# Four layers on one core: values turned by VectorE and through DRAM, values' products one projection later, position tables stationary with the queries moving

## Time and profile before

| | |
|---|---|
| median of 3 runs | 1244.69 us (1243.16 to 1244.88) |
| the profiled execution, its own time | 1246.36 us |
| its span | 1244.4 us |
| PE / PEld busy | 1216.4 us (98%) / 975.0 us (78%) |
| DVE / ACT / POOL busy | 690.4 us (55%) / 475.1 us (38%) / 641.5 us (52%) |
| chain that ended last | PE 89%, DVE 5%, ACT 2% |
| DMA | 155.03 MB, mean 125 GB/s |

### The profile page before, as it was taken

One profiled execution on the slowest core, in us unless ns is written; L12 is line 12 of the kernel. 1 busy time (PEld: TensorE's weight loads), 2 busy tenths in 40 slices (PEclk: granted clock), 3 DMA queues, 4 the chain that ended last, 5 costly groups with the idle time before them and its releaser, 6 DMA issues.

```text
span 1244.4 us, 19555 instructions
## 1 busy us (share of the span) xinstructions
PE 1216.4 (98%) x6768; PEld 975.0 (78%) x6768; DVE 690.4 (55%) x1434; ACT 475.1 (38%) x1229; POOL 641.5 (52%) x726
## 2 busy tenths in 40 slices
PE   6999999999999999999999999999999999889998
PEld 4788896478888888888888878777887787668887
DVE  7534444775665433666452578756347776476212
ACT  3611141034645320656341164644206555243212
POOL 4633389256565567555546655555665556464000
PEclk9999999999999999999999999999999999999999
DMA  5211124025564643454645356557535565620012
GB/s 185 84 46 48 34 56 117 8 65 160 154 169 137 184 134 97 127 177 128 185 136 166 86 160 212 180 160 223 168 102 151 175 209 156 205 60 1 29 40 68
DMA packets 129376, 155.03 MB, mean 125 GB/s; under 512 B 30080, under 2 KB 84000, under 8 KB 129280
## 3 DMA queue, kind: packets, MB, share of 16 engines
q1 hardware_dynamic: 118976, 146.92, 39.7%
q10 hardware_dynamic: 10304, 6.88, 1.8%
HBM read 111.81 MB, written 37.75 MB: 120 GB/s over the span
## 4 chain that ended last, share of the span: by engine, by line
PE 89%; DVE 5%; ACT 2%; issue 1%; DMA 1%; SPq 1%; POOL 0%; ACTq 0%; DVEq 0%; POOLq 0%
PE PS L1137 53%; PE PS L682 7%; PE PS L1758 7%; PE PS L1183 4%; PE PS L960 3%; PE PS L969 2%; PE PS L975 2%; PE PS L1227 2%; PE PS L1216 2%; PE PS L1775 2%; PE PS L1247 2%; PE PS L665 1%; PE PS L1197 1%; DVE bst L257 1%; PE PS L700 1%
## 5 line engine op out<-in xcount | busy, mean ns | idle before, releaser
L1137 PE MATMUL PS<-XB,w_hi 128*128 128x512 f32 x1024 | 340.5, 397 | 1.2 <-POOL w_lo L228 1.2
L226 POOL CAST w_hi<-w_raw 128x512 fp32r<-128x512 f32 x195 | 124.2, 637 | 307.5 <-PE PS L1137 213.0
L228 POOL TENSOR_TENSOR w_lo<-w_raw,w_hi 128x512 fp32r<-128x512 f32 x195 | 256.1, 1313 | 15.6
L1137 PEld LDWEIGHTS PS<-XB,w_hi 128*128 128x128 f32 x1024 | 192.2, 188 | 47.1 <-issue 5.0
L1137 PE MATMUL PS<-XB,w_lo 128*128 128x512 f32 x512 | 200.2, 391 | 0.0
L1137 PE MATMUL PS<-XB,part 128*128 128x512 f32 x768 | 190.3, 394 | 0.0
L1137 PEld LDWEIGHTS PS<-XB,part 128*128 128x128 f32 x768 | 141.9, 188 | 32.2 <-issue 2.3
L1373 ACT ACTIVATE part<-PS,nmax 128x256 f32<-128x256 f32 (+1 forms) x256 | 112.2, 443 | 141.6 <-DVE nmax L1485 93.2
L1383 ACT ACTIVATE part<-part,prec 128x256 f32<-128x256 f32 (+1 forms) x256 | 105.8, 476 | 27.7 <-DVE prec L1500 27.7
L228 POOL TENSOR_TENSOR part<-part,part 128x512 fp32r<-128x512 f32 x85 | 111.5, 1312 | 6.8
L1137 PE MATMUL PS<-part,w_hi 128*128 128x512 f32 x344 | 112.9, 395 | 1.5 <-DVE part L1544 1.5
(11 more groups left out here) (136 smaller groups left out, 1884.0 us busy)
## 6 DMA issues: line engine op xcount, KB each, us to landing
w_raw<-in_w SPq DMA_DIRECT2D x187, 256.0 KB, 2.8
part<-in_w SPq DMA_DIRECT2D x85, 256.0 KB, 2.8
turned<-part SPq DMA_DIRECT2D x128, 128.0 KB, 2.9
part<-turned SPq DMA_DIRECT2D x32, 512.0 KB, 5.0
turned<-part SPq DMA_DIRECT2D x128, 96.0 KB, 2.5
part<-turned SPq DMA_DIRECT2D x32, 384.0 KB, 4.0
strips<-part ACTq DMA_DIRECT2D x16, 256.0 KB, 2.7
out_x<-xT SPq DMA_DIRECT2D x16, 256.0 KB, 2.1
```

The source lines that it names most:

```text
L226: pool.tensor_copy(hi, raw).then_inc(w_hi_done, 1)
L228: pool.tensor_tensor(lo, raw, hi.bitcast(F32), ALU.subtract).then_inc(w_ready, 1)
L1137: m = nc.tensor.matmul(PS[:, bank, :], wt[:, (c % 4) * P:(c % 4) * P + P], rhs(hl, c), start=c == k == 0, stop=c == CK - 1 and k == 2)
```

## The change

- Values: PE's four transposes per item (32 items) go, and so does ACT's copy in front of them. DVE transposes the values from PSUM in 32 x 32 squares (`turn_values`), SP writes them to a new DRAM tensor in four DMAs and reads them back in one (`values_to_dram`, `values_from_dram`), and ACT copies them into `v` (`take_v`), within the next item. The bias of the values in layer 2 is added after their product instead.
- Order on PE: keys of i + 1, values of i, values' product of i - 1, queries of i + 2, and the eight output blocks after these queries instead of before them. Weights are listed in that order.
- Position products: 24 matmuls of 64 columns per item of layer 2 become three of 512 columns, the tables stationary and the queries moving in permuted order. The result lies with positions on the partitions. DVE transposes it (`turn_relative`) and ACT stores it in four DMAs instead of one, right behind the first exponentials; its two copies L1407 go.
- `rest_of_o` and `evac_o` stand behind the normalization, `norm.coefficients` moves from j = 0 to j = 1; at j = 0 the queries of i + 2 are read out ahead of the output blocks' sums.
- Probabilities go out in four DMAs per item instead of eight, of twice the size, and come back in two.
- The end: six output blocks instead of three are begun ahead of the last values' product, in six banks, and `build_m` has other banks and places (`M_AFTER`).

```diff
--- before.py
+++ after.py
             take_block(i, "V", range(0 if i else 1, 2))
+            if i + 2 < ITEMS:
+                take_block(i + 2, "Q")
             if s and j == 0:
                 for o in range(CK):
                     take((s - 1, "O", o), STAGES[s - 1][0], "O", o)
-            if i + 2 < ITEMS:
-                take_block(i + 2, "Q")
-            for o in {ITEMS - 2: (0,), ITEMS - 1: (1, 2)}.get(i, ()):
...
-    vT = carve(13312, [P, HALF])
+    vB = carve(13312, [P, 4 * P])
...
-    probB = [carve(at, [P, 4 * N]) for at in (14848, 11264)]
+    probB = carve(11264, [P, 8 * N])
...
-        def turn_values(i):
-            pe.wait_ge(v_evac, i + 1)
-            if turned_bank(i) == S:
-                pe.wait_ge(p_exp, 4 * i + 1)
-            else:
-                pe.wait_ge(rel_evac, 2 * (ITEMS - LO_KEYS))
-            if i:
-                pe.wait_ge(v_ready, i)
-            for tt in range(4):
-                m = nc.tensor.transpose(PS[:, turned_bank(i), tt * P:tt * P + P], vT[:, tt * P:tt * P + P], ident[:, :])
-            m.then_inc(v_tr, 1)
...
             if i == ITEMS or layer_of(i) == 1:
                 return
             pe.wait_ge(q_hi, i + 1)
             pe.wait_ge(q_lo, i + 1)
...
             pe.wait_ge(tables_ready, 1)
-            for tt in range(4):
-                for k, (x, y) in enumerate(((qh[i % 2], rel_hi), (qh[i % 2], rel_lo), (ql[i % 2], rel_hi))):
-                    for hh in range(2):
-                        rows = slice(64 * hh, 64 * hh + 64)
-                        to = PS[:, REL[hh], 64 * tt:64 * tt + 64].rearrange("p (t n) -> p t n", t=2)
-                        m = nc.tensor.matmul(to, x[rows, tt * P:tt * P + P], y[rows, :, 32 * hh:32 * hh + 32],
-                                             start=k == 0, stop=k == 2)
-                        if (tt, k) == (3, 2):
-                            m.then_inc(rel_done, 1)
+            for k, (x, y) in enumerate(((rel_hi, qh[i % 2]), (rel_lo, qh[i % 2]), (rel_hi, ql[i % 2]))):
+                m = nc.tensor.matmul(PS[:, X, :], x.rearrange("p r n -> p (r n)"), y.rearrange("p (a y x) -> p y a x", a=2, y=SIDE),
+                                     start=k == 0, stop=k == 2)
+            m.then_inc(rel_done, 1)
...
+        project(2, "Q", range(CK))
         for i in range(1, LAST - 1):
             score_block(i)
             project(i + 1, "K", range(CK))
+            project(i, "V", range(CK))
             attend(i - 1, 0)
             attend(i - 1, 1)
-            project(i, "V", range(CK))
+            project(i + 2, "Q", range(CK))
             if i % PAIRS == 0:
                 s = i // PAIRS - 1
-                out_block(s, 0, range(CK))
-                out_block(s, 1, range(0, 2))
-                turn_values(i)
-                out_block(s, 1, range(2, CK))
-                for o in range(2, CK):
+                for o in range(CK):
                     out_block(s, o, range(CK))
-                project(i + 2, "Q", range(CK))
-            else:
-                project(i + 2, "Q", range(0, 2))
-                turn_values(i)
...
         score_block(i)
         project(LAST, "K", range(CK))
+        project(i, "V", range(CK))
         attend(i - 1, 0)
         attend(i - 1, 1)
-        project(i, "V", range(CK))
         scores(LAST, 0)
         scores(LAST, 1)
-        out_block(3, 0, range(0, 2))
-        turn_values(i)
-        out_block(3, 0, range(2, 4))
+        out_block(3, 0, range(0, 4))
         project(LAST, "V", range(CK))
+        for o in (1, 2):
+            out_block(3, o, range(0, 4))
         attend(i, 0)
         attend(i, 1)
-        out_block(3, 1, range(0, 4))
-        turn_values(LAST)
...
-        for o in range(3):
-            out_block(3, o, range(4, 7))
+        for o in (3, 4, 5):
+            out_block(3, o, range(0, 4))
         attend(LAST, 0)
         attend(LAST, 1)
-        for o in range(3):
-            out_block(3, o, range(7, CK))
+        for o in range(6):
+            out_block(3, o, range(4, CK))
             for k in M_AFTER[o, 1]:
                 build_m(k)
-        for o in range(3, CK):
...
-        def evac_v(i):
...
+        def take_v(i):
+            act.wait_ge(v_in, 16 * (i + 1))
...
-                act.wait_ge(v_tr, i)
...
+                act.wait_ge(o_done, 2 * i)
+            dst = v.rearrange("p t (b c) -> p t b c", b=4)
+            nc.scalar.activation(dst, vB.rearrange("p (b t c) -> p t b c", b=4, t=4), ACT.Copy).then_inc(v_ready, 1)
...
-        def evac_relative(i):
...
-            for hh in range(2):
-                act.wait_ge(rel_done, 2 * (i - LO_KEYS) + hh + 1)
-                nc.scalar.activation(all_rel[:, :, :, hh, :],
-                                     PS[:, REL[hh], 0:4 * 64].rearrange("p (t a n) -> p t a n", t=4, a=2), ACT.Copy).then_inc(rel_evac, 1)
-            strips_to_dram(act, i)
...
         for i in range(ITEMS):
             j, s = i % PAIRS, i // PAIRS
-            if i:
+            if i and (i < PAIRS or j != 1):
                 evac_q(i + 1)
             exps(i, 0)
+            if LO_KEYS <= i + 1 < ITEMS:
+                strips_to_dram(act, i + 1)
             exps(i, 1)
             normalize(i, 0)
             normalize(i, 1)
-            evac_relative(i + 1)
+            if 0 < i < LAST:
+                take_v(i - 1)
             exps(i, 2)
             normalize(i, 2)
+            if i == LAST:
+                take_v(i - 1)
...
             evac_k(i + 1)
-            if j:
-                evac_o(i - 1)
-            evac_v(i)
...
                     norm.head(s + 1, c)
+            if i:
+                evac_o(i - 1)
+            if i and j == 0:
+                evac_q(i + 2)
+        take_v(LAST)
...
-        def take_v(i):
-            dve.wait_ge(v_tr, i + 1)
+        def turn_values(i):
+            product_done(dve, (i, "V"))
             if i:
-                dve.wait_ge(o_done, 2 * i)
-            nc.vector.tensor_copy(v.rearrange("p a n -> p (a n)"), PS[:, turned_bank(i), :]).then_inc(v_ready, 1)
+                dve.wait_ge(v_ready, i)
+            src = PS[:, bank_of(i, "V"), :].rearrange("p (t q c) -> p t q c", t=4, q=4)
+            dst = vB.rearrange("p (q t c) -> p t q c", q=4, t=4)
+            nc.vector.transpose(dst, src).then_inc(v_turned, 1)
...
+        def turn_relative(i):
+            if i == ITEMS or layer_of(i) == 1:
+                return
+            dve.wait_ge(rel_done, i - LO_KEYS + 1)
+            if i > LO_KEYS:
+                dve.wait_ge(strips_out, 64 * (i - LO_KEYS))
+            nc.vector.transpose(all_rel, PS[:, X, :]).then_inc(rel_evac, 1)
...
             s, j = i // PAIRS, i % PAIRS
-            if i:
+            if i and (i < PAIRS or j != 1):
                 rest_of_q(i + 1)
             sum_relative(i, 0)
             sum_relative(i, 1)
             maxima(i, 0)
+            turn_relative(i + 1)
...
-            if i and j == 0:
-                rest_of_o(i - 1)
...
             invert_sums(i, 3)
             turn_probs(i, 3)
             if i < LAST:
                 rest_of_k(i + 1)
-            if j:
+            if i < LAST:
+                turn_values(i)
...
+                rest_of_q(i + 2)
                 for o in range(CK):
                     add_out(s - 1, o)
...
-            if j or i == 0:
-                take_v(i)
-            if j == 0:
+            if j == 1:
                 norm.coefficients(s + 1)
             if 1 <= j <= 4:
                 for c in (2 * j - 2, 2 * j - 1):
                     norm.y(nc.vector, s + 1, c)
                 for c in (2 * j - 2, 2 * j - 1):
                     norm.rest(s + 1, c)
+            if j:
+                rest_of_o(i - 1)
         rest_of_o(LAST)
         for o in range(CK):
...
-        sp.wait_ge(rel_evac, 2 * done + 2)
-        whole = strips[buf].rearrange("(t p) n -> p t n", p=P)
-        sp.dma_start(whole, all_rel[:, :, :, :, :].rearrange("p t a b n -> p t (a b n)")).then_inc(strips_out, 16)
+        sp.wait_ge(rel_evac, done + 1)
+        rows = strips[buf].rearrange("(ax y) n -> ax y n", y=SIDE)
+        for b in range(4):
+            src = all_rel[32 * b:32 * b + 32, :].rearrange("p (y n) -> p y n", y=SIDE)
+            sp.dma_start(rows[:, :, 32 * b:32 * b + 32], src).then_inc(strips_out, 16)
...
+    def values_to_dram(sp, i):
+        sp.wait_ge(v_turned, i + 1)
+        if i >= 2:
+            sp.wait_ge(v_in, 16 * (i - 1))
+        for b in range(4):
+            to = bass.AP(values.tensor, (i % 2) * P * 4 * P + P * b, [[4 * P, 32], [32 * 4 * P, 4], [1, P]])
+            sp.dma_start(to, vB[32 * b:32 * b + 32, :].rearrange("p (q r) -> p q r", q=4)).then_inc(v_out, 16)
+    def values_from_dram(sp, i):
+        sp.wait_ge(v_out, 64 * (i + 1))
+        sp.dma_start(vB, values[i % 2, :, :]).then_inc(v_in, 16)
+    STRIPS_AT = [slots[(i + 1, "K"), 1] if i < LAST else slots[(i, "V"), 0] for i in range(ITEMS)]
```

(12 more changed lines are left out.)

169 lines of the change are left out of this document (88 added, 81 removed).

## The result

| | before | after |
|---|---|---|
| median of the runs shown with the result (lowest to highest), us | 1244.69 (1242.74 to 1245.58) | 1252.31 (1249.91 to 1257.06) |
| ratio to before, 95% interval | 1 | 1.0069 (1.0050 to 1.0088) |
| profiled execution, us (span) | 1246.36 (1244.4) | 1252.31 (1250.5) |

A forecast was written before the change was run, and what follows sets the result against it. PE bounds the kernel, with the round of DVE and ACT 1.5 us behind. PE's savings 26.6 - 22.0 of waiting + 8.5 at the end = 13.1 us, from 1244.7 to 1231 us; range 1214 to 1243.

The forecast's parts named there:

- What PE loses: PE in layers 1 and 2: dropped transposes save 14.1 us, shorter position products 12.5 us, together 26.6 us.
- What DVE and ACT gain: Layer 2: ACT's four strip issues take 2.3 us, the round becomes 22.8 us, PE's waiting gives back 22.0 us.
- rival 2: Dear ACT strip issues, S for four: slower above S = 3.8 us, 1262 us at 1.25 us each; chance 0.13.
- The step that failed: ACT's new copy of the values, `take_v`, stands where ACT waited for maxima anyway; no cost was given.
- Queues: Extra transfers on SP and the DMA engines cost nothing; SP needs about 13.4 of 21 us per layer 2 item.
- The end: From the scores of item 31 to layer 3: 61 us, 12 us less; net gain 8.5 us.
- The clock: At the end, the wait of some 3.4 us before the scores of 31 may lower the clock: 1.5 us.
- Rival 4: SP or the DMA engines hold back weights in layer 2, 8 to 15 us: 1239 to 1247; chance 0.10.
- Rival 1: ACT's strip issues are cheap, 0.37 us each: waiting 15.6 us, gain 20 us, 1224 us; chance 0.20.
- Rival 3: Strips land late: from 12 us on every layer 2 item waits, at 16 us 1291 us; chance 0.05.

The follow-up runs named there:

- experiment 3: Against the kernel after the change: DVE turns the values earlier and they go through DRAM ahead of the probabilities; strips stay on ACT; 1237.42 us.
- experiment 9: Against the kernel before: only the position products take the new form, with four stores on ACT; values, order and end as before; 1247.68 us.
- experiment 6: From experiment 3: DVE's second step of the next stage's normalization moved behind the next item's second maxima; 1234.53 us.
- experiments 17 and 18: Two of the strips' four stores on ACT, two on POOL: 17 from experiment 3, 1223.35 us; 18 from experiment 6, 1222.36 us.
- 5: From the kernel after the change: values of all items but the last two turned on PE again, without DRAM; 1245.67 us.

## Why the prediction was wrong

**What PE loses: right.** Layer 1 repeats every 19.94 us and layer 2 at PE's bound every 21.04, within 0.1 us of the working. The permuted moving operand costs next to nothing: from the start of the three matmuls (748.38) to the next product's (749.17) go 0.79 us, against 0.68.

**What DVE and ACT gain: the mechanism right, the sum by luck.** PE did wait ahead of L1227, 19.5 us in all where 22.0 were worked out: 3.07 and three times 2.78 us in one stage, 4.26 and 3.83 in the other, for 5.45 and three times 1.85 in each. But with the values early and the issues still on ACT (experiment 3) it is 9.6 us, so half of the 19.5 went with the places of the values' steps, which the working did not have. The four issues took not 2.3 us but 3.4 on average (4.0 in the item shown), a mis-sized term; by rival 2's formula that alone makes 10 us. In experiment 9, without the values in DRAM, they took 2.6 us in most items. The DMA engines' share beside them was 0.60 to 0.71 there and 0.85 to 1.02 in the kernel after, where the prediction's rows of eight issues had 0.59 and 0.15: rows from quieter moments were poor neighbours. The share is not all of it, since at 0.95 some bursts took 2.8 us and another 4.8.

**The step that failed** is the sentence that ACT's new copy stands where ACT waited for maxima anyway, with the one under "Queues" that costs SP at nothing. I worked out what the transfers' issues take of SP, but not when their result is due. The stores of the values stand behind those of the probabilities, the load behind two other loads, and ACT takes them ahead of the third exponentials. The way took 16.9 us, and ACT came for them after 15.4 (734.29 - 1.43 - 717.44); in the item shown at 852.39 it waited 4.45 us and PE's values' product with it. The term that was put at nothing is the difference between experiment 3 and the kernel after: 14.9 us.

**Where the miss lies.** Between the profiled executions the kernel lost 5.9 us, where 13.1 of gain were forecast: 19 us off. Up to item 17 it was 11.2 us ahead, where 17 x 0.47 + 0.83 = 8.8 was worked out. Items 17 to 31: 13 x 0.47 + 14 x 0.83 = 17.7 us less work, 22.0 given back and the scores of 31 starting 2.0 later made 6.3 of loss; measured 23.8. The end: 6.8 us of gain for 10.5 (12 less 1.5 for the clock). So 17.5 us of the miss are in layer 2's items and nearly 4 in the end. PE's rows account for the 17.5: 2.5 less than worked out at L1227, 9.4 at L1200 and 2.1 more at L1179 that the working did not have, and an estimated 8.8 for the clock behind these waits. Experiment 3 took 17.6 back in the same items. In the medians the miss is 20.7 us, 14.9 for the values and 5.8 that experiment 3 still has. This split depends on the order of the steps, since the dearer issues and the values' way meet in the same items.

**The clock.** I took its loss into account at the end only. In layer 2 it came with the longer waits. PE's timeline and windows (PEclk is the last number but two) of the kernel after:

```profile
956.03 1.62 PE L1227 MATMUL PS<-part,part 128*128 128x512 f32 x3 [4.26 <-issue]
```

```profile
956.00:959.00 3.00, 2.97 (x7) 2.42 (x8) 2.96 (x5) 0.50 (x3) 0.00 (x0) 0.50 0.77 213
959.00:962.00 3.00, 3.00 (x8) 2.32 (x8) 2.03 (x5) 0.52 (x3) 0.00 (x0) 0.50 0.91 268
962.00:965.00 3.00, 3.00 (x14) 2.39 (x14) 0.65 (x2) 2.33 (x8) 1.91 (x2) 0.98 1.00 256
```

Behind the wait of 2.78 us (the row at 748.38) the same view has

```profile
749.00:752.00 3.00, 3.00 (x15) 2.46 (x14) 2.96 (x5) 1.02 (x4) 0.00 (x0) 1.00 0.91 261
```

The item with the first wait took 28.13 us (950.08 to 978.21): 21.04 of work, 4.26 of waiting and 2.8 for the clock. The item with the second took 23.80, 21.04 + 2.78, nothing for the clock. The length of the wait alone does not say which it will be. A wait of 2.40 us at `attend` was followed by the lower clock:

```profile
1063.33 2.56 PE L1200 MATMUL PS<-part,part 128*64 128x256 f32 x16 [2.40 <-issue]
```

```profile
1064.00:1067.00 3.00, 1.89 (x12) 0.84 (x8) 2.25 (x5) 2.06 (x8) 0.00 (x0) 0.59 0.18 38
```

The items with waits of 3.07, 3.21 and 3.83 us took some 1.6 us more than work and wait each; so the 3 us in the expectation of experiment 6 hold for the waits at L1227 that it had in view, and no further. The 8.8 us above are these five: 1.5, 1.7, 1.6, 2.8 and, behind the 2.40 us, 1.2.

**The end: 4 us off.** 66.4 us from the scores of 31 to layer 3, 73.1 before and 61 forecast, 62.5 with the clock. The scores of 31 waited 3.68 us, near the worked out 3.4, but the clock behind that wait was at 0.52 over 6 us, some 2.8 us instead of the 1.5 taken.

**The rivals.** None had the values' late return. Rival 4 named SP and a time of 1239 to 1247 us, but by way of weights, which were late for 1.4 us in all. Rival 2 (dear issues) had its break-even at 3.8 us for the four: they took 3.4 on average, so by its own formula the change would still have gained 3 us. Rival 1's 1224 us for cheap issues is what experiments 17 and 18 reached, with the issues cheap and the values early; with the values late no run here tests it. Rival 3 did not happen: the stores landed in 5.5 us and DVE waited for no strips.

**How the parts add up**, in us against the kernel before: position products alone +2.8 (experiment 9); with the new order and end, values on PE, 0 to +0.5 (5); with the values through DRAM as written +7.6 (after), values first -7.5 (3), stores shared -21.2 (17).

## What to carry to other kernels

When a step moves from the bounding engine to a way through DRAM, write down the clock time of each station of its way (ready, stored, loaded, taken), in the order of the queue that carries it; a queue whose issues fit in the period can still deliver late. Where two rounds have nearly the same length, look at what the other one does when one is cut: without ACT's issues its waits for the values grew from 67.9 to 107.3 us, and the kernel gained only 2.5. And a burst of DMA issues on an engine of the critical round can be worth sharing: here two queues were better than either ACT or POOL alone.

## What was unexpected

- How much PE's waits differ in price: 2.8 us of clock (0.50 is 1.2 GHz) on top of a wait of 4.26 us, 1.6 on top of 3.83, none on top of 2.78, some 1.2 on top of 2.40. The item with the wait of 3.07 us at 723.02 took 25.65 us (718.26 to 743.91), 1.5 more than work and wait. In experiment 3 two waits of the same 3.40 us cost 2.8 and 1.6.
- The same four transfers took 2.6 us of ACT's queue in most items of experiment 9 (up to 3.6), 3.4 on average after (2.7 to 4.8). Two on ACT and two on POOL took 1.2 us on each queue.
- Stored by POOL, the strips of all items were 2048 packets; ACT's queue after had 35648, and 1856 were left on it when POOL stored them. The Trainium skill (page "Trainium Kernel Development and Optimization", section "Key Constraints") says that issuing from several engines only saves their time for issuing. The runs agree as far as they show it: ACT's share fell from 3.2 us an item on average (experiment 3) to 1.2 (experiment 17), and the kernel's time by 14.1 us.
- Joined to one transfer, the four stores cost 0.53 us to issue and 14.8 us until they could be read.
